# Attention and routed experts on one core: the step from the routing tables to the experts' first steps, reordered on VectorE and ScalarE

## The reference

```
x = layernorm(x + fourier_attention(x))      # chunks of 64 tokens, real FFT, attention on the low
                                             # frequencies, a causal convolution on the high ones
d2   = |x|^2 + |centroid|^2 - 2 x centroid.T # distance to E=8 centroids
w, sel = top_k(sqrt(max(d2, 1e-12)), K=2)    # the two farthest
w    = softmax(w)
out  = sum over the two chosen experts e of  w_e * ((silu(x Wg[e] + bg[e]) * (x W1[e] + b1[e])) W2[e] + b2[e])
x = layernorm(x + out)
```

## Time and profile before

| | us |
|---|---|
| median of three executions | 565.73 |
| lowest, highest | 564.67, 567.99 |
| the profiled execution, its own time | 564.46 |
| its span (first to last instruction) | 562.6 |
| TensorE busy in the span | 503.3 |
| VectorE, ScalarE, GpSimd busy | 363.9, 349.3, 293.3 |

### The profile page before, as it was taken

The page is one execution under the profiler, slowest core; times in us unless marked ns, Lnnn a source line. Parts: engine busy times, 40 slices in busy tenths (PEclk is TensorE's granted clock), DMA queues, the critical chain, the costliest instruction groups (busy, mean ns, idle before and its releaser), DMA issues.

```text
span 562.6 us, 13552 instructions
## 1 busy us (share of the span) xinstructions
PE 503.3 (89%) x3988; PEld 479.5 (85%) x3988; DVE 363.9 (65%) x1045; ACT 349.3 (62%) x744; POOL 293.3 (52%) x424
## 2 busy tenths in 40 slices
PE   4677988988989776899999999999999999999990
PEld 4575977977977665799999999999999999999980
DVE  3778798898898899534344465564646456666763
ACT  3565778888788565465555556666565656755651
POOL 0152544645635446454535455777776777754453
PEclk9979999999999965699999999999999999999996
DMA  8350264164153014100000001111111111100000
GB/s 226 121 129 10 69 157 126 53 164 130 50 158 91 2 46 52 24 22 22 16 22 17 21 17 31 31 40 31 40 30 42 34 37 35 34 20 16 20 30 28
DMA packets 47183, 31.56 MB, mean 56 GB/s; under 512 B 12123, under 2 KB 44710, under 8 KB 47126
## 3 DMA queue, kind: packets, MB, share of 16 engines
q1 hardware_dynamic: 42214, 21.77, 15.1%
q0 software_dynamic: 4096, 8.66, 5.6%
q10 hardware_dynamic: 816, 0.41, 0.3%
HBM read 22.13 MB, written 8.69 MB: 55 GB/s over the span
## 4 chain that ended last, share of the span: by engine, by line
PE 56%; DVE 4%; ACT 1%; issue 1%; POOL 0%; DVEq 0%; ACTq 0%
PE ps L1656 26%; PE ps L1681 18%; PE ps L1671 9%; PE ps L1665 1%; DVE xT L1310 1%; PE ps L1237 1%; POOL out_dram L1617 0%; ACT xT L1230 0%; DVE xs L1860 0%; DVEq L1586 0%; ACT L1764 0%; PE ps L1497 0%; DVE y L1827 0%; DVE ya L1823 0%; DVE yb L1825 0%
## 5 line engine op out<-in xcount | busy, mean ns | idle before, releaser
L1656 PE MATMUL ps<-wts,xh 128*128 x620 | 154.5, 333 | 0.0
L1847 DVE TENSOR_TENSOR h<-ps,sg 128x684 f32<-128x684 f32 x78 | 67.6, 866 | 90.0 <-PE ps L1656 82.3
L1634 POOL TENSOR_TENSOR xl<-xT,xh 127x128 fp32r<-127x128 f32 x155 | 68.0, 458 | 100.5 <-ACT xh L1750 100.4
L1681 PE MATMUL ps<-w2s,hT 115*128 (+1 forms) x930 | 116.6, 275 | 0.3 <-DVE xs L1860 0.3
L1681 PEld LDWEIGHTS ps<-w2s,hT 115*128 115x128 f32 (+1 forms) x930 | 110.0, 191 | 0.6 <-issue 0.6
L1656 PEld LDWEIGHTS ps<-wts,xh 128*128 128x128 f32 x620 | 104.8, 191 | 0.2
L1656 PE MATMUL ps<-wts,xl 128*128 x310 | 99.7, 321 | 0.0
L1764 ACT ACTIVATE sg<-ps 128x684 f32<-128x684 f32 x78 | 57.6, 739 | 66.2 <-PE ps L1656 66.2
L1773 ACT ACTIVATE hT<-ps 114x768 f32<-114x768 f32 x78 | 62.9, 806 | 55.9 <-PE ps L1671 55.9
L1860 DVE SCALAR_TENSOR_TENSOR xs<-ps,xs 128x128 f32 x155 | 54.4, 351 | 50.9 <-PE ps L1681 48.0
L1617 POOL DMA_INDIRECT out_dram<-xs,idx x64 | 62.8, 982 | 26.1 <-issue 17.6
(11 more groups left out here) (290 smaller groups left out, 840.9 us busy)
## 6 DMA issues: line engine op xcount, KB each, us to landing
xt<-_attn_hidden_states_dram SPq DMA_DIRECT2D x8, 512.0 KB, 6.1
xres<-_attn_hidden_states_dram SPq DMA_DIRECT2D x7, 512.0 KB, 5.2
rows_dram<-x1s SPq DMA_DIRECT2D x7, 512.0 KB, 3.7
w2s<-in_L_ffn_W_dram SPq DMA_DIRECT2D x8, 171.0 KB
st<-in_L_ffn_Wg_dram SPq DMA_DIRECT2D x8, 171.0 KB, 2.3
st<-in_L_ffn_W_dram SPq DMA_DIRECT2D x8, 171.0 KB, 2.4
stl<-in_L_ffn_Wg_dram SPq DMA_DIRECT2D x8, 171.0 KB, 3.3
stl<-in_L_ffn_W_dram SPq DMA_DIRECT2D x8, 171.0 KB, 4.0
```

What stands on the lines that cost most here:

```text
L1634: v.tensor_tensor(xl[0:D - 1, i % 2, u, :], xT[0:D - 1, bass.ds(off[u], P)], xh[0:D - 1, i % 2, u, :].bitcast(F32), ALU.subtract).then_inc ...
L1656: mm = pe.matmul(ps[:, 2 * w + u, 0:HF], a[:, t % 2, u, :], wflat[:, bass.ds(w1[u] + (b + w * HF), HF)], start=(k == 0), stop=(k == 2))
L1681: mm = pe.matmul(ps[:, low(t) + u, 0:D], hT[0:n, t % 2, u, k, :], w2flat[0:n, bass.ds(w1[2 + u] + k * D, D)], start=(k == 0), stop=(k == 2))
L1847: v.tensor_tensor(h[:, t % 2, 0:units(t), :], ps[:, 2:2 + units(t), 0:HF], sg[:, 0:units(t), :], ALU.mult).then_inc(s["h_done"], 1)
```

## The change

1. `later_places(2)` is moved in front of the units' table on VectorE, and `later_high(2)` on ScalarE in front of the first step. `later_places(3)` stays behind the table's first part.
2. The table is read from PSUM in one copy of 468 elements in place of 156, and its fields are made in two parts, with `tabled` raised after each. Offsets of rows and weights (fields 2 and 4), which only VectorE reads, are in the second part, and VectorE waits for it before step 0's accumulation.
3. ScalarE runs a Silu on the two columns of `bb`, a tensor that nobody reads any more, behind `hihot1` and ahead of `later_high(0)`; Silu's table load stands there now.
4. On ScalarE the late Exp and its plus-one come before the fourth `turned` and `bb`, and VectorE's late reciprocal (L1315) comes before its wait for `places`.
5. `mask32` is made by ScalarE at the end of the first half, and GpSimd's copy goes, with the wait for it.

```diff
@@ first half, ScalarE, tail
+                act.wait_ge(rest_in, 16)
+                nc.scalar.activation(g["mask32"][:, :, :], g["short"]("mask", BR).unsqueeze(2).broadcast_to((BR, CT, NCH * BLK * 2)), ACT.Copy)
@@ route, VectorE
-            dve.wait_ge(s["mask"], 1)
...
+            dve.wait_ge(s["sum"], 2)
+            v.reciprocal(w1[:, TE:NT], dn[:, TE:NT]).then_inc(s["share"], 1)
 
             dve.wait_ge(s["places"], 1)
...
-            dve.wait_ge(s["sum"], 2)
-            v.reciprocal(w1[:, TE:NT], dn[:, TE:NT]).then_inc(s["share"], 1)
             low_places(0)
...
-            later_places(0)
-            later_places(1)
+            for c in range(3):
+                later_places(c)
...
-            link(v.tensor_copy(ut[:, :], ps[0:1, 6, 0:UPAD]))
-            uexp, uwt = unit(ps[0:1, 6, UPAD:2 * UPAD]), unit(ps[0:1, 6, 2 * UPAD:3 * UPAD])
-            v.tensor_scalar(fields(0), unit(ut[:, :]), float(P), None, ALU.mult)
-            v.tensor_scalar(fields(2), unit(ut[:, :]), float(ROW), None, ALU.mult)
+            link(v.tensor_copy(ut[:, :], ps[0:1, 6, 0:3 * UPAD]))
+            utile, uexp, uwt = (unit(ut[:, f * UPAD:(f + 1) * UPAD]) for f in range(3))
+            v.tensor_scalar(fields(0), utile, float(P), None, ALU.mult)
             v.tensor_scalar(fields(6), uexp, float(WE), None, ALU.mult)
-            v.tensor_scalar(fields(8), uexp, float(3 * D), None, ALU.mult)
-            link(v.tensor_scalar(ut[:, :], ut[:, :], float(ROW), float(D + E), ALU.mult, ALU.add))
-            v.tensor_tensor(fields(4), uwt, unit(ut[:, :]), ALU.add).then_inc(tabled, 1)
-            later_places(2)
+            v.tensor_scalar(fields(8), uexp, float(3 * D), None, ALU.mult).then_inc(tabled, 1)
             later_places(3)
+            v.tensor_scalar(fields(2), utile, float(ROW), None, ALU.mult)
+            link(v.tensor_scalar(utile, utile, float(ROW), float(D + E), ALU.mult, ALU.add))
+            v.tensor_tensor(fields(4), uwt, utile, ALU.add).then_inc(tabled, 1)
@@ route, ScalarE
-            turned(EARLY, 0)
-            act.wait_ge(s["bounds"], 1)
-            nc.scalar.activation(bb[:, :], bounds, ACT.Copy).then_inc(s["bounds_cp"], 1)
             act.wait_ge(s["difference"], 1)
             nc.scalar.activation(ew[:, TE:NT], df[:, TE:NT], ACT.Exp).then_inc(s["exp"], 1)
             act.wait_ge(s["exp"], 2)
             nc.scalar.activation(dn[:, TE:NT], ew[:, TE:NT], ACT.Copy, bias=1.0).then_inc(s["sum"], 1)
+            turned(EARLY, 0)
+            act.wait_ge(s["bounds"], 1)
+            nc.scalar.activation(bb[:, :], bounds, ACT.Copy).then_inc(s["bounds_cp"], 1)
             scaled(TB // 2, TB)
...
-            later_high(act, 0)
-            later_high(act, 1)
+
+            nc.scalar.activation(bb[:, :], bb[:, :], ACT.Silu)
+            for c in range(3):
+                later_high(act, c)
@@ route, GpSimd
-            v.tensor_copy(mask32[:, :, :], short("mask", BR).unsqueeze(2).broadcast_to((BR, CT, NCH * BLK * 2))).then_inc(s["mask"], 1)
@@ experts, ScalarE
                     if i == 0:
-                        later_high(act, 2)
                         later_high(act, 3)
@@ experts, VectorE
+                if c == 0:
+                    dve.wait_ge(tabled, 2)
```

More of the change, by code:

```diff
@@ L220, in program @@
         yl, nl = (sb(k, [P, TB]) for k in ("yl", "nl"))
+        mask32 = sb("mask32", [BR, CT, NCH * BLK * 2], BF16)
         rows_out, rest_in, bias_out, last_out, w_early = (ctx.enter_context(nc.semaphore(k)) for k in ("rows_out", "rest_in", "bias_out", "last_out", "w_early"))
@@ L1123, in phase2 @@
         uhot = ctx.enter_context(nc.sbuf_tensor("uhot", [P, 4, UPAD], BF16))
-        ut = ctx.enter_context(nc.sbuf_tensor("ut", [1, UPAD], F32))
+        ut = ctx.enter_context(nc.sbuf_tensor("ut", [1, 3 * UPAD], F32))
         inv2 = ctx.enter_context(nc.sbuf_tensor("inv2", [P, 2 * NT], F32))
@@ L1181, in route @@
     rows_t, xh, xl, hT, prep = (g[k] for k in ("rows_t", "xh", "xl", "hT", "prep"))
-    lohot, hihot2, hieq2, uhot, ut, inv2, xt, yl, nl, last_out = (g[k] for k in ("lohot", "hihot2", "hieq2", "uhot", "ut", "inv2", "xt", "yl", "nl", "last_out"))
+    lohot, hihot2, hieq2, uhot, ut, inv2, xt, yl, nl, mask32, last_out = (g[k] for k in ("lohot", "hihot2", "hieq2", "uhot", "ut", "inv2", "xt", "yl", "nl", "mask32", "last_out"))
     OH, zb, onesb, oh1, oh2, m1, m2 = (g[k] for k in ("OH", "zb", "onesb", "oh1", "oh2", "m1", "m2"))
@@ L1198, in route @@
         R = sb("R", [BR, CT, NCH, BLK, 2], BF16)
-        mask32 = sb("mask32", [BR, CT, NCH * BLK * 2], BF16)
         mxs = sb("mxs", [64, P])
@@ L1221, in route @@
             "chain", "late", "one_hot", "counts", "counts_cp", "tri", "tri_cp", "turned", "turned_cp", "totals", "totals_cp", "firsts", "bounds", "bounds_cp",
-            "split", "present", "places", "need", "need_cp", "upto", "unit_hot", "tables", "high", "high_place", "high_tile", "hot", "inverse", "mask", "ranks", "last_x1",
+            "split", "present", "places", "need", "need_cp", "upto", "unit_hot", "tables", "high", "high_place", "high_tile", "hot", "inverse", "ranks", "last_x1",
             "high2", "high2_place", "high2_tile", "inverse2",
```

## The result

The changed kernel takes 562.47 us, the median of 19 executions (559.96 to 564.75); the kernel before, run beside it, 566.52 (563.93 to 567.99, 19 executions). The ratio is 0.9929, 95% interval 0.9914 to 0.9943: 0.7% or 4.0 us faster. The prediction had 562.0, which is 3.7 less than 565.73. The profiled execution takes 561.65 us, its span is 559.8, against 564.46 and 562.6.

What follows compares the result with a forecast made beforehand. TensorE alone was taken to bound every step from step 3, so reaching step 1 sooner moves the end. Gains 1.87 + 0.16 + 0.26 + 1.40 = 3.69 us off the 565.73 median gave 562.0 us, range 560.4 to 564.3.

Steps and rivals of the forecast that it cites:

- Third quarter sooner: TensorE between tile 0's transpose and the later inverse's third quarter: the wait for ScalarE's `hihot2` half goes, gain 1.87 us.
- The clock: TensorE in step 0 and the fourth quarter: once risen the clock stays full, 3.96 us instead of 5.36, gain 1.40.
- the load, 0.26: Silu's 1.28 us table load on ScalarE moves into idle time before the routing's end; TensorE's 0.26 us wait before step 1 goes.
- Rival B: TensorE around step 0: hole goes, but clock rises late or falls again; 563.4 us, or 562.7 with half the gain; chance 0.28.
- Late reciprocal, 0.16: VectorE's routing chain: the reciprocal moves into a wait, gain 0.16 us.
- `mask32`, 0: ScalarE makes the mask while waiting ahead of the routing; cost 0, or about 0.60 us without that cover.
- The table hidden by 0.5: Ahead of step 0: the later units' table lets `xh` finish at 232.3 us, before TensorE needs it at 232.85; cost 0.
- signs of being wrong: TensorE waiting at step 0's `up` for `xh` or at step 1 for a gather, or a longer routing chain before 226 us.
- Gathers, 0: GpSimd's first gather starts once the index list is there, and its transfer was not on the chain; gain 0.
- rival C: Steps 1 and 2: tile 3's gather or ScalarE's chain late by up to 1 us; gain 2.7, 563.0 us; chance 0.08.
- A: The whole change as summed, every term holding: 562.0 us; chance 0.57.
- Rival D: ScalarE before the fourth `turned`: a load twice as long makes Exp delay it, 0.5 us reaching TensorE; 562.5 us; chance 0.02.

Runs made afterwards that it cites:

- the first two experiments: Kernel before with only the third quarter moved ahead: 561.5 us, ratio 0.9931; changed kernel with only that move undone: 565.0 us, ratio 0.9996.
- the table experiment: Kernel with gathers of tiles 3 and 4 issued ahead of `xl`, plus the units' table in one part again, six field instructions before `tabled`: 561.79 us, ratio 0.9937.
- the changed kernel's second profile: The changed kernel run again with nothing altered: 561.67 us, ratio 0.9934 to the kernel before.

## Why the prediction was right, and where its terms were not

The time, the direction and the size came out: 562.47 against 562.0, within 560.4 to 564.3. The mechanism, the hole with the clock behind it, was right; that the sum came so near is in part luck, since two gains that I had missed stand against two losses that I had put at nothing. By steps, with what the traces gave in brackets:

- *Third quarter sooner, 1.87* (1.87: step 0 from 8.36 to 6.49 us behind the index list). Right, and shown from both sides by the first two experiments. That it agrees to a hundredth is chance: the third quarter itself starts 2.09 us sooner (6.84 to 4.75 behind the index list), but from its start to step 0 it is 1.74 us in place of 1.52, with the clock still at half until 232.14 and `xh` ready only at 233.14.
- *The clock, 1.40, with the load, 0.26.* From step 0 to step 1 the sum was 1.66; measured is 1.87 (5.64 to 3.77). That the clock, once risen, would stay without the hole is confirmed in all eleven profiles without it, for step 0. Rival B, a late or lost rise in step 0, did not occur in any of these eleven executions; the others' aren't known. Behind the rise the Trainium skill ("TensorE: Matmul & The Clock Gate", the section on the HAM clock gate) has a monitor that runs freely, so that its moment would differ between executions; in twelve of thirteen profiles it came 4.6 to 5.6 us behind the index list, once at 2.4. It varies, as the page says, but in none of them did it come as late as step 0's start, at 6.3 us or later.
- *The load, 0.26 in the old order, more in the new.* The reasoning that both edits belong together was right, but its price was too small: I gave only the new order's delay, 1.3 at ScalarE, and the experiments show 1.1 at step 1, and in two profiles up to 1.8 more by a clock that falls behind TensorE's idle microsecond.
- *Late reciprocal, 0.16* (0.00). The step that failed is "I take 0, with 0.3 either way" for GpSimd's arithmetic beside VectorE: it took just that 0.16 back.
- *`mask32`, 0* (0.41). I looked for cover on ScalarE, and there it is hidden. I did not look at what its removal from GpSimd does to VectorE: the first routing instruction had taken 0.73 us beside that copy, and is on the chain.
- *The table hidden by 0.5* (by nothing). The register load was put at the median of 78, 0.49; the first one takes 0.69 (the chain of the table experiment shows it), and from `tabled` to the first `xT` ScalarE takes 1.03. One of the prediction's own signs of being wrong, that TensorE waits at `up` of step 0 for `xh`, is there in small: 0.12 us between the third quarter's end (231.43 + 1.62) and 233.17. The copy was right, 0.64 against 0.63.
- *Gathers, 0, and rival C.* A wait came, 0.84 us at step 2 between the two kernels, and for tile 4, not tile 3. The margin was worked out with 2.6 to 2.9 from issue to landing, and this one gather takes 3.5 to 3.8. C was priced at up to 1 us and given a chance of 0.08; it took 0.84 off the sum, left the rest of A standing, and came in all four profiles with this order and Silu's load early (TensorE idle 0.43 to 0.91 us). The step that failed is the 0.6 of margin, which had no term for a packet of another queue.
- *Rival D.* The load's end and the next instruction are 0.01 us apart here too (214.13 + 1.28, Exp at 215.42), so the drain of 1.38 us in the Trainium skill ("ScalarE: Activation LUTs", What ACT_TABLE_LOAD costs) isn't seen, and the fourth `turned` started in time.

In all, 0.41 that I had not counted and 0.21 too little at the clock stand against 0.84 of gather wait and 0.16 of reciprocal: 3.69 + 0.62 - 1.00 is 3.31. The stretch says 3.19, since 0.12 more went between steps 2 and 3, and in the changed kernel's second profile 3.64, with half of the gather wait.

## What to carry to other kernels

Where an engine starts a long, steady loop, count the idle time ahead of it twice, once as delay and once for the clock that may fall behind it: here putting back a hole of under 2 us cost 3.3 by step 1 (13.55 against 10.26), and an idle microsecond ahead of step 1 cost up to 2.9 by step 3 where the clock fell, and no more than its delay where it didn't. When work is taken off an engine that had time for it, look at what shared its time, not at the engine itself. And where the times spread by more than the change is worth, measure the stretch between two instructions that the change can't move.

## What the runs showed of the hardware that I had not expected

A gather of 128 rows lands 2.5 to 2.9 us after its issue, but 2.8 to 4.4 us, median 3.7, in the 41 of 496 cases in which a 16 KB packet of the instruction queue was in flight as its own packets started. VectorE's 128x128 operation took 0.73 us beside a GpSimd copy of 112x512 and 0.29 without it, the same in every profile of either kind. Nine matmuls of 448 columns in the idle time of the routing did not bring the clock's rise forward, while with TensorE idle for 1.0 us ahead of step 1 it fell in two profiles of three.
